# Two attention layers on one core: first half of the next queries ahead of a step's first score, maxima at scores 1 to 8, residual additions behind all maxima

## The chip, the core and the metric

One Trainium2 chip, one of its NeuronCores. The engines are TensorE (PE, matmuls), VectorE (DVE), ScalarE (ACT), GpSimd (POOL) and SyncE (SP, which here only issues DMAs). The metric is the time of one execution on the device in microseconds; lower is better.

## The reference

Four layers over x, which is 4 x 1024 rows of 256 numbers, each added to x behind a layer norm: a cross-attention over 77 context rows with a mask and 16 heads, a mixture of six small experts, a second cross-attention over the same context with one key and value head for all 16 query heads, and a feed-forward layer. Cut to the two attentions, which the change touches, the masked one first, then the scores of the second:

```python
q = (h @ Wq.T + bq).reshape(B, N, H, D).transpose(0, 2, 1, 3)
scores = jnp.einsum('bhnd,bhtd->bhnt', q, k) * scale + attention_mask[:, None, :, :]
attn = jax.nn.softmax(scores, axis=-1)
out = jnp.einsum('bhnt,bhtd->bhnd', attn, v)
return out.transpose(0, 2, 1, 3).reshape(B, N, C) @ Wo.T + bo

attn_score = jnp.einsum('bhid,bjd->bhij', qh, k) / np.sqrt(D_HEAD)
attn_prob = jax.nn.softmax(attn_score, axis=-1)
```

## The kernel before

**Tiling.** The 4096 rows of x are cut into 8 blocks of 512. Each attention is a loop of 8 steps G, one for a block: G = 0 to 7 is the masked layer (here also steps 0 to 7), G = 8 to 15 the second one. Between them the experts run, behind them the feed-forward layer. The order on each engine is written out by hand in one program for each engine, and the engines meet by semaphores.

**One step.** A step does 16 scores, one for a head. `score` (L383) multiplies keys by a stack of queries in SBUF, `qst`, which holds the high and low parts of the queries and, in two rows, the row maxima, so that the matmul gives scores with the maximum already taken off; the masked layer adds the mask by a second matmul (L399). ScalarE's `exp` (L297) follows each. After each group of four heads `weigh` (L402) multiplies by the values, eight matmul records in the trace, and `divide` (L330) on VectorE transposes the result and divides it by its denominator: L335, L338, L340. The fourth group of a step is weighed and divided in the next step. `fold` (L343) transposes a half of the heads, `lead_quotient` (ScalarE) and `rest_quotient` (GpSimd) split it into a high and a low part, and `output` (L412) multiplies it by Wo in twelve matmuls (L421), for two halves k of the block; `add` (L348) adds each to x. All that is work for the block p = G-1.

For the next block n = G+1 the same step prepares the stack. `queries` (L357) computes one half c of its queries in six matmuls (L135). It waits for the rest `xl` of the normalized input, both halves. ScalarE's `leading` (L283) takes the high part, VectorE's `rest` (L310) the low part, and SP copies both into `qst` (`stack_queries`, L242). Then the maxima: 16 units u, each one matmul (two in the masked layer, L371 and L374) of 128 queries by the keys of four heads (`max_unit`, L361), reduced by VectorE (`take_maxima`, L320, L327). The units share two banks, `X`:

```python
if u >= len(banks):
    pe.wait_ge(self.max_taken, 16 * G + u - len(banks) + 1)
```

When all 16 are reduced, TensorE transposes them (`turn_maxima`, L377), ScalarE copies them (`maxima`, L292) and SP copies them on into `qst` (`stack_maxima`, L253, qst<-mt). Score 0 of the next step waits for that DMA:

```python
if i == 0:
    pe.wait_ge(self.mt_stacked, 16 * (G + 1))
```

For the block after that, nm = G+2, VectorE takes the moments of its rows (`moments`, L87, at the start of a step), GpSimd the inverse root (`invert`), ScalarE normalizes (`norm`, at score 9), TensorE transposes (`turn`, L118, at scores 11 and 12, each behind the residual addition `att.added` that frees its bank `W`), ScalarE takes the high part (`lead`, L124), VectorE the rest (L130), which ends just at the step's end.

**Order before, TensorE.** score i; at i = 0 and 1 the queries' halves behind the score; at 1 the fourth weighing of p; at 3 to 10 two units each; at 8 and 9 the outputs; at 5, 9 and 13 the weighings; at 12 the transposition of the maxima; at 11 and 12 the input's. **VectorE:** moments, two rests of the queries, maxima 0 to 3, division 3 and fold 1 of p, maxima 4 to 9, division 0, maxima 10 and 11, the two additions, maxima 12 to 15, division 1, fold 0, two rests of the input, division 2. In step 11 (BLOCKS + 3) VectorE also prepares bias rows of the feed-forward layer (L1371 to L1380). In steps 9, 10, 12 and 13 ScalarE and GpSimd split weights of the feed-forward layer in passing (L1045, L1053). The last step of each layer has no queries and no maxima.

## Time and profile before

| | us |
|---|---|
| median of 3 runs (lowest, highest) | 865.36 (864.72, 866.4) |
| the profiled execution | 866.98 |
| its span in the profile | 865.2 |
| busy: PE, DVE, ACT, POOL | 774.8 (90%), 659.9 (76%), 520.1 (60%), 398.4 (46%) |

The kernel runs through the masked attention from about 41 to 232 us, the experts to about 440, the second attention to about 632 and the feed-forward layer behind it. A step of the masked layer takes some 26.3 us, one of the second some 23.4 to 24.5. In a timeline each row is an instruction or a run of equal ones: start, duration, engine, line, what it writes and reads, and in brackets how long its engine had been idle and what released it. Matmuls overlap: one of 512 columns starts every 0.23 us and is shown with 0.39 to 0.40; one that had to wait for its operands is shown longer. A number of bank or buffer is left out of the names; "bank" is PSUM.

### The profile page before, as it was taken

Reading aid. Unit: us, or ns where it says so; the run is one execution under the profiler, and the core shown is the slowest. Engines: PE = TensorE matmul, PEld = TensorE weight load, DVE = VectorE, ACT = ScalarE, POOL = GpSimd, SP = SyncE. Lnnn points to the kernel's source line nnn. Section 1 sums busy time; section 2 is a strip of 40 time slices with the busy share of each in tenths; the row PEclk is TensorE's granted clock in tenths of the full one; section 3 lists DMA queues with packets and bytes.
Section 4 is the critical chain, followed back from the end, with each engine's and each line's share of the span. In section 5 each row is a group of like instructions: output and inputs, shape, how many; then the busy total and the mean of one; then the engine's idle time right before and its main releaser. Section 6 shows DMA issues by size and latency. Waiting matters only on the chain.

```text
span 865.2 us, 13721 instructions
## 1 busy us (share of the span) xinstructions
PE 774.8 (90%) x4452; PEld 568.9 (66%) x4452; DVE 659.9 (76%) x1576; ACT 520.1 (60%) x942; POOL 398.4 (46%) x323
## 2 busy tenths in 40 slices
PE   4799999999899999999988988988879999899996
PEld 3456556666467787777754544554458888788885
DVE  7657877777768777877777888888777778787784
ACT  3455565555554455544446675666668787788774
POOL 5523322223233433443311221222159998988995
PEclk9999999999999999999988999999999999999999
DMA  6965643355200000001075446555000000000001
GB/s 216 159 164 109 146 78 72 74 107 102 70 0 1 2 3 5 2 1 50 15 97 70 59 60 110 88 75 75 3 1 1 25 1 26 25 25 2 25 25 50
DMA packets 24817, 48.01 MB, mean 55 GB/s; under 512 B 3655, under 2 KB 6856, under 8 KB 24234
## 3 DMA queue, kind: packets, MB, share of 16 engines
q1 hardware_dynamic: 23224, 46.02, 27.8%
q10 hardware_dynamic: 1522, 1.11, 0.4%
q8 instruction: 37, 0.61, 0.3%
q14 instruction: 34, 0.28, 0.1%
HBM read 11.47 MB, written 4.19 MB: 18 GB/s over the span
## 4 chain that ended last, share of the span: by engine, by line
PE 52%; DVE 18%; POOL 11%; issue 7%; ACT 5%; DMA 5%; POOLq 0%; ACTq 0%; DVEq 0%
PE bank L135 15%; PE bank L396 5%; PE bank L371 5%; PE bank L629 5%; PE bank L421 5%; DMA qst<-mt 4%; PE bank L407 4%; DVE mx L327 4%; POOL eex L508 4%; PE bank L777 4%; POOL fy L696 3%; POOL frise L689 3%; PE bank L399 2%; PE bank L121 2%; DVE x L597 2%
## 5 line engine op out<-in xcount | busy, mean ns | idle before, releaser
L301 ACT ACTIVATE pt<-bank 77x512 f32<-77x512 f32 x256 | 146.4, 589 | 123.5 <-PE bank L399 76.4
L327 DVE TENSOR_REDUCE mx<-bank 128x4 f32<-128x308 f32 x256 | 108.9, 471 | 30.3 <-PE bank L374 17.8
L396 PE MATMUL bank<-qst,l_kst 128*77 128x512 f32 (+1 forms) x256 | 106.7, 431 | 19.3 <-DMA qst<-mt 13.3
L696 POOL TENSOR_TENSOR fy<-fpart,fg 128x512 f32<-128x512 f32 x64 | 103.9, 1624 | 9.4 <-DVE fpart L737 4.8
L371 PE MATMUL bank<-l_kblk,qh 128*128 128x308 f32 x256 | 89.7, 366 | 12.0 <-DVE mx L327 9.8
L689 POOL TENSOR_TENSOR frise<-fg,fg 128x512 f32<-128x512 f32 x64 | 90.1, 1408 | 9.0 <-POOL fy L696 4.7
L103 POOL TENSOR_TENSOR rstd<-var,minus_half 128x4 f32<-128x4 f32 x32 | 33.2, 1039 | 127.6 <-DVE var L98 74.9
L396 PEld LDWEIGHTS bank<-qst,l_kst 128*77 128x77 f32 (+1 forms) x256 | 36.8, 148 | 83.2 <-issue 48.8
L277 POOL TENSOR_TENSOR ol<-ot,oh 128x512 fp32r<-128x512 f32 x32 | 43.0, 1345 | 94.2 <-ACT oh L306 62.1
L371 PEld LDWEIGHTS bank<-l_kblk,qh 128*128 128x128 f32 x256 | 49.3, 193 | 55.9 <-issue 46.8
L737 DVE SCALAR_TENSOR_TENSOR fpart<-ffixed,frise 128x512 f32<-128x512 uint16 x64 | 58.6, 915 | 33.0 <-POOL frise L689 32.8
L597 DVE SCALAR_TENSOR_TENSOR x<-bank,eweight,x 128x256 f32<-128x256 f32 x192 | 79.5, 475 | 4.4 <-PE bank L629 4.1
L777 PE MATMUL bank<-fw2h,fyh 128*128 128x256 f32 x256 | 72.3, 282 | 3.5 <-DVE fyl L743 3.5
L407 PE MATMUL bank<-pt,l_vall 128*32 128x512 f32 x512 | 69.4, 614 | 6.4 <-DVE ut L335 3.8
L113 ACT ACTIVATE xn<-x,shift,rstd 128x256 f32<-128x256 f32 x128 | 68.1, 590 | 11.6 <-POOL shift L105 11.6
L777 PE MATMUL bank<-fw2l,fyh 128*128 128x256 f32 x256 | 71.9, 281 | 0.0
L777 PE MATMUL bank<-fw2h,fyl 128*128 128x256 f32 x256 | 71.8, 281 | 0.0
L706 ACT ACTIVATE fg<-ffixed 128x512 f32<-128x512 int16 x64 | 40.4, 632 | 45.4 <-DVE ffixed L731 45.2
L629 PE MATMUL bank<-ew2h,ehh 128*128 128x256 f32 x192 | 56.6, 295 | 10.3 <-DVE x L597 10.3
L629 PE MATMUL bank<-ew2l,ehh 128*128 128x256 f32 x192 | 54.7, 285 | 0.0
L629 PE MATMUL bank<-ew2h,ehl 128*128 128x256 f32 x192 | 54.5, 284 | 0.0
L731 DVE TENSOR_SCALAR ffixed<-bank 128x512 int32<-128x512 f32 x64 | 43.7, 683 | 12.0 <-PE bank L135 11.9
(179 smaller groups left out, 2144.2 us busy)
## 6 DMA issues: line engine op xcount, KB each, us to landing
qst<-qh SPq DMA_DIRECT2D x64, 256.0 KB, 6.7
qst<-ql SPq DMA_DIRECT2D x32, 256.0 KB, 9.0
out<-x SPq DMA_DIRECT2D x8, 512.0 KB, 2.6
qst<-ml SPq DMA_DIRECT2D x8, 480.0 KB
x<-in_x SPq DMA_DIRECT2D x3, 1024.0 KB, 12.7
weights<-in_mlp_w SPq DMA_DIRECT2D x2, 1024.0 KB, 5.1
mraw<-in_mask SPq DMA_DIRECT2D x8, 154.0 KB
x<-in_x SPq DMA_DIRECT2D x2, 512.0 KB, 5.5
```

Source lines behind the costliest of these rows:

```text
L113: last = self.nc.scalar.activation(self.xn[:, t:t + 1, :], self.tile(n, t), ACT.Identity, bias=self.shift[:, t, :], scale=self.rstd[:, t, :])
L135: last = self.nc.tensor.matmul(out, w, a, start=(first and k == 0), stop=(k == len(ops) - 1))
L301: self.nc.scalar.activation(self.pt[0:T, i // 4 % 2, i % 4, :], self.bank_of(G, i)[0:T, :], ACT.Exp).then_inc(self.probs, 1)
L327: self.nc.vector.reduce_max(out, banks[u % len(banks)][:, 0:4 * T].rearrange("q (p par t) -> q p par t", p=2, par=2), AX.X).then_inc(self. ...
L371: last = self.nc.tensor.matmul(bank, self.qh[:, c, tile], keys, start=True, stop=not layer.masked)
L396: last = self.nc.tensor.matmul(out, layer.kst[rows, layer.stack(c * HC + 2 * k + par), b * T:(b + 1) * T], self.qst[rows, self.slot(G), c ...
L407: last = self.nc.tensor.matmul(self.U[32 * k:32 * k + 32, :], layer.vall[:, self.batch(G), layer.value(c * HC + 2 * k + par), :], self.pt[ ...
L597: last = self.nc.vector.scalar_tensor_tensor(tile, part, self.weight[:, g % 2, 2 * k + t, e:e + 1], tile, ALU.mult, ALU.add)
L629: last = self.nc.tensor.matmul(self.OUT[k][:, t * D:(t + 1) * D], a[:, e % self.R, tile], w[:, e, :], start=(j == 0), stop=(j == 2))
L689: self.nc.gpsimd.tensor_tensor(self.rise[:, k % 2, :], self.g1[:, k % self.R, :], self.g0[:, k % self.R, :], ALU.subtract).then_inc(self.r ...
L696: self.nc.gpsimd.tensor_tensor(self.y[:, k % 2, :], self.part[:, k % 2, :], self.g0[:, k % self.R, :], ALU.add).then_inc(self.y_ready, 1)
L777: last = nc.tensor.matmul(self.OUT[2 * (g % 2) + t // 2][:, t % 2 * D:(t % 2 + 1) * D], a[:, k % self.R, t * P:(t + 1) * P], w[:, c, :], s ...
```

## The change

The same instructions on the same data, in another order on three engines, in both layers:

- TensorE: `queries` c now stands ahead of score c instead of behind it (c = 0, 1). The units stand at scores 1 to 8 instead of 3 to 10, and ahead of the fourth weighing at score 1. The transposition of the maxima stands at score 10 instead of 12.
- ScalarE: `leading` stands ahead of the exponential of the same number, and `maxima` at 10 instead of 12.
- VectorE: maxima 0 and 1 stand between the two rests of the queries; maxima 4 and 5 between division 3 and fold 1; all of 10 to 15 behind division 0; and both residual additions behind all maxima.

SP's and GpSimd's programs are unchanged. The part of the masked layer; the second layer's is the same but for its names and limits:

```diff
@@ -1105,9 +1105,9 @@
                 for G in range(BLOCKS):
                     p, n, nm = G - 1, G + 1, G + 2
                     for h in range(H):
-                        att.exp(act, G, h)
                         if h < C and n < BLOCKS:
                             att.leading(act, n, h)
+                        att.exp(act, G, h)
                         if h == 3 and p >= 0:
                             if p == 0:
                                 act.wait_ge(kblk_more, H)
...
@@ -1276,23 +1276,24 @@
                     if n < BLOCKS:
                         for c in range(C):
                             att.rest(dve, n, c)
-                        att.take_maxima(dve, n, range(0, 4), att.X)
+                            att.take_maxima(dve, n, range(2 * c, 2 * c + 2), att.X)
                     if p >= 0:
                         att.divide(dve, p, 3)
+                    if n < BLOCKS:
+                        att.take_maxima(dve, n, range(4, 6), att.X)
+                    if p >= 0:
                         att.fold(dve, p, 1)
                     if n < BLOCKS:
-                        att.take_maxima(dve, n, range(4, 10), att.X)
+                        att.take_maxima(dve, n, range(6, 10), att.X)
                     else:
                         ex.split_w1(dve, ew1)
                     att.divide(dve, G, 0)
                     if n < BLOCKS:
-                        att.take_maxima(dve, n, range(10, 12), att.X)
+                        att.take_maxima(dve, n, range(10, 16), att.X)
                     if p >= 0:
                         for k in range(2):
                             att.add(dve, p, k)
-                    if n < BLOCKS:
-                        att.take_maxima(dve, n, range(12, 16), att.X)
-                    else:
+                    if n == BLOCKS:
                         ex.split_w2(dve)
                         ex.split_router(dve)
                     att.divide(dve, G, 1)
...
@@ -1456,16 +1458,16 @@
                     for i in range(H):
                         if G == 0 and i == HC:
                             pe.wait_ge(kst_in[1], 16 * 6)
-                        att.score(pe, l0, G, i)
                         if i < C and n < BLOCKS:
                             att.queries(pe, l0, n, i)
+                        att.score(pe, l0, G, i)
+                        if 1 <= i <= 8 and n < BLOCKS:
+                            if i == 1 and G == 1:
+                                pe.wait_ge(kblk_more, H)
+                            for u in (2 * (i - 1), 2 * (i - 1) + 1):
+                                att.max_unit(pe, l0, n, u, att.X)
                         if i == 1 and p >= 0:
                             att.weigh(pe, l0, p, 3)
-                        if 3 <= i <= 10 and n < BLOCKS:
-                            if i == 3 and G == 1:
-                                pe.wait_ge(kblk_more, H)
-                            for u in (2 * (i - 3), 2 * (i - 3) + 1):
-                                att.max_unit(pe, l0, n, u, att.X)
                         if i in (8, 9) and p >= 0:
                             if G == 1 and i == 8:
                                 pe.wait_ge(wol_ready, 1)
@@ -1478,7 +1480,7 @@
                             att.output(pe, l0, p, i - 8)
                         if i in (5, 9, 13):
                             att.weigh(pe, l0, G, i // 4 - 1)
-                        if i == 12 and n < BLOCKS:
+                        if i == 10 and n < BLOCKS:
                             att.turn_maxima(pe, n, att.X[0])
                         if i in (11, 12) and nm <= BLOCKS:
                             if p >= 0:
```

## Rows read from the trace of the kernel before

**Rows 1.** The page's chain that ended last: share of the span by line

```profile
PE bank L135 15%; PE bank L396 5%; PE bank L371 5%; PE bank L629 5%; PE bank L421 5%; DMA qst<-mt 4%; PE bank L407 4%; DVE mx L327 4%; POOL eex L508 4%; PE bank L777 4%; POOL fy L696 3%; POOL frise L689 3%; PE bank L399 2%; PE bank L121 2%; DVE x L597 2%
```

**Rows 2.** Waits of 40 to 232 us: engine line waited for: us, times, longest

```profile
PE bank L396 <- DMA qst<-mt: 5.2, 7, 0.8
```

**Rows 3.** The waits, 445 to 632 us (second attention)

```profile
PE bank L396 <- DMA qst<-mt: 8.1, 6, 1.4
```

**Rows 4.** Timeline, TensorE, masked layer: start, us, engine, line, out<-in, count [idle before]

```profile
144.98 0.46 PE L396 MATMUL bank<-qst,l_kst 128*77 128x512 f32 x1 [0.75 <-DMA qst<-mt]
...
159.11 0.39 PE L416 MATMUL bank<-bias,ones 128*128 128x512 f32 x1
...
163.53 1.06 PE L407 MATMUL bank<-pt,l_vall 128*32 128x512 f32 x8
```

**Rows 5.** Timeline, VectorE, masked layer, the same step

```profile
143.39 0.69 DVE L130 TENSOR_TENSOR xl<-bank,xh 128x512 fp32r<-128x512 f32 x1 [0.26 <-ACT xh L126]
...
169.73 0.69 DVE L130 TENSOR_TENSOR xl<-bank,xh 128x512 fp32r<-128x512 f32 x1 [0.27 <-ACT xh L126]
```

**Rows 6.** Busy us (instructions) of each engine in one step, clock, DMA share, GB/s

```profile
564.65:588.03 23.38, 20.92 (x112) 11.75 (x112) 19.87 (x48) 15.47 (x30) 6.31 (x7) 1.00 0.53 70
```

**Rows 7.** Timeline, TensorE, one step of the second layer

```profile
564.65 0.46 PE L396 MATMUL bank<-qst,l_kst 98*77 98x512 f32 x1 [1.37 <-DMA qst<-mt]
...
575.49 0.76 PE L371 MATMUL bank<-l_kblk,qh 128*128 128x308 f32 x2
...
576.53 0.77 PE L371 MATMUL bank<-l_kblk,qh 128*128 128x308 f32 x2
577.14 0.28 PE L421 MATMUL bank<-l_woh,oh 128*128 128x256 f32 x1
...
580.97 1.07 PE L407 MATMUL bank<-pt,l_vall 128*32 128x512 f32 x8
```

**Rows 8.** The chain of that step in order: start us, us, what

```profile
561.69 2.92 DMA qst<-mt
...
565.12 1.38 PE bank L135 x6
```

**Rows 9.** Timeline, VectorE, the same step of the second layer

```profile
563.13 0.69 DVE L130 TENSOR_TENSOR xl<-bank,xh 128x512 fp32r<-128x512 f32 x1 [0.27 <-ACT xh L126]
...
564.76 1.14 DVE L340 TENSOR_TENSOR o<-ut,rden 128x256 f32<-128x256 f32 x1
565.83 1.40 DVE L90 BATCH_NORM_STATS2 stats<-x 128x6 f32<-128x256 f32 x4
...
567.83 0.68 DVE L317 TENSOR_TENSOR ql<-bank,qh 128x512 fp32r<-128x512 f32 x1
...
571.74 0.71 DVE L335 STREAM_TRANSPOSE ut<-bank 128x512 f32<-128x512 f32 x1
...
572.77 0.43 DVE L340 TENSOR_TENSOR o<-ut,rden 128x256 f32<-128x256 f32 x1
...
586.54 0.69 DVE L130 TENSOR_TENSOR xl<-bank,xh 128x512 fp32r<-128x512 f32 x1 [0.26 <-ACT xh L126]
```

**Rows 10.** TensorE in two stretches: busy us (instructions), granted clock, DMA share, GB/s

```profile
452.00:454.00 2.00, 2.00 (x10) 0.69 1.06 131
480.00:482.00 2.00, 2.00 (x9) 0.52 1.08 127
```

**Rows 11.** Timeline, TensorE, start of step 0

```profile
40.87 0.68 PE L396 MATMUL bank<-qst,l_kst 128*77 128x512 f32 x1 [4.22 <-issue]
```

**Rows 12.** Timeline, VectorE, before step 0

```profile
36.88 1.29 DVE L130 TENSOR_TENSOR xl<-bank,xh 128x512 fp32r<-128x512 f32 x2 [6.16 <-ACT xh L126]
```

**Rows 13.** Timeline, GpSimd, step 0

```profile
45.11 1.03 POOL L263 TENSOR_TENSOR mh<-mraw,zero 77x512 fp32r<-77x512 f32 x1
```

**Rows 14.** Timeline, TensorE, the starts of steps 8 and 9

```profile
445.20 0.43 PE L396 MATMUL bank<-qst,l_kst 98*77 98x512 f32 x1 [1.55 <-issue]
...
467.73 0.46 PE L396 MATMUL bank<-qst,l_kst 98*77 98x512 f32 x1 [1.34 <-DMA qst<-mt]
```

More of the change, by code:

```diff
@@ L1120, in _ @@
                             norm.norm(act, nm)
-                        if h == 12 and n < BLOCKS:
+                        if h == 10 and n < BLOCKS:
                             att.maxima(act, n, att.X[0])
@@ L1174, in _ @@
                     for h in range(H):
-                        att.exp(act, G, h)
                         if h < C and n < 2 * BLOCKS:
                             att.leading(act, n, h)
+                        att.exp(act, G, h)
                         if h == 3 and p >= BLOCKS:
@@ L1183, in _ @@
                             norm.norm(act, nm)
-                        if h == 12 and n < 2 * BLOCKS:
+                        if h == 10 and n < 2 * BLOCKS:
                             att.maxima(act, n, att.X[0])
@@ L1353, in _ @@
                             att.rest(dve, n, c)
-                        att.take_maxima(dve, n, range(0, 4), att.X)
+                            att.take_maxima(dve, n, range(2 * c, 2 * c + 2), att.X)
                     if p >= BLOCKS:
                         att.divide(dve, p, 3)
+                    if n < 2 * BLOCKS:
+                        att.take_maxima(dve, n, range(4, 6), att.X)
+                    if p >= BLOCKS:
                         att.fold(dve, p, 1)
                     if n < 2 * BLOCKS:
-                        att.take_maxima(dve, n, range(4, 10), att.X)
+                        att.take_maxima(dve, n, range(6, 10), att.X)
                     att.divide(dve, G, 0)
                     if n < 2 * BLOCKS:
-                        att.take_maxima(dve, n, range(10, 12), att.X)
+                        att.take_maxima(dve, n, range(10, 16), att.X)
                     if p >= BLOCKS:
@@ L1365, in _ @@
                             att.add(dve, p, k)
-                    if n < 2 * BLOCKS:
-                        att.take_maxima(dve, n, range(12, 16), att.X)
                     if G == BLOCKS + 3:
@@ L1559, in _ @@
                             pe.wait_ge(ex.added, ALL_EXP)
-                        att.score(pe, l1, G, i)
                         if i < C and n < 2 * BLOCKS:
                             att.queries(pe, l1, n, i)
+                        att.score(pe, l1, G, i)
+                        if 1 <= i <= 8 and n < 2 * BLOCKS:
+                            for u in (2 * (i - 1), 2 * (i - 1) + 1):
+                                att.max_unit(pe, l1, n, u, att.X)
                         if i == 1 and p >= BLOCKS:
                             att.weigh(pe, l1, p, 3)
-                        if 3 <= i <= 10 and n < 2 * BLOCKS:
-                            for u in (2 * (i - 3), 2 * (i - 3) + 1):
-                                att.max_unit(pe, l1, n, u, att.X)
                         if i in (8, 9) and p >= BLOCKS:
@@ L1575, in _ @@
                             att.weigh(pe, l1, G, i // 4 - 1)
-                        if i == 12 and n < 2 * BLOCKS:
+                        if i == 10 and n < 2 * BLOCKS:
                             att.turn_maxima(pe, n, att.X[0])
```

## The prediction

> **What bounds the kernel now.** I read the chain of work that ended last first: TensorE heads it by its matmuls, but the copy of the maxima into the query stack (qst<-mt) holds 4% of it and the maxima on VectorE (L327) another 4% [rows 1]. The waits then say what that copy costs: TensorE stood idle for it 7 times in the masked layer, 5.2 us in all, and 6 times in the second, 8.1 us [rows 2, 3]. So a step begins with 0.75 us (masked) or 1.37 us (second layer) of idle TensorE in front of score 0 [rows 4, 7]. That is what the change aims at. The busy times of one step of the second layer are to be read beside it: of 23.38 us VectorE works 19.87 and TensorE's "20.92" is stretched by matmuls that wait [rows 6]. VectorE has 3.5 us to spare in a step, and what a reordering is worth depends on where in the step they lie.
>
> **The head of a step.** The first half of the queries (L135, six matmuls, 1.38 us [rows 8]) needs only the rest of the normalized input, which VectorE ends at 563.13+0.69 = 563.82; score 0 starts at 564.65 [rows 7, 9]. With the queries first, TensorE starts at about 563.87 (0.05 from release to start, an estimate; bounds 0 and 0.2): 0.8 us earlier. In the masked layer it is 143.39+0.69 = 144.08 against 144.98 [rows 4, 5]: 0.85. The copy itself is issued two scores earlier, behind score 10, and 1.6 us of queries now run before score 0, so its 2.9 us [rows 8] are hidden: by the walk below unit 15 is issued at 15.2, the transposition of the maxima behind score 10 ends at 20.0, ScalarE's copy at 20.9, the transfer at 23.9, and score 0 wants it at 25.4. SP's queue does not oppose that: the copy stands behind the query copies and the mask load there, all issued in the step's first third. What is late next at the head is VectorE's rest itself, which a step's end sets.
>
> **The maxima at scores 1 to 8.** Each of the 16 units writes one of two banks and must wait until VectorE has reduced the unit two before. Where nothing else lies between, that loop of two units and a score takes 1.04 us (575.49 to 576.53), of which TensorE needs 0.24 for the score and 0.3 for the units [rows 7]. Before, 12 units precede the first output (577.14) and the last four lie behind outputs, where VectorE has had time and they go at TensorE's pace. After, all 16 precede it, without filler: queries, the fourth weighing of the step before and the first weighing lie among them, no output.
>
> I walk one step of the second layer, from its start 0 (queries first). TensorE: queries 1.39, score 0.24, queries, score, units 0 and 1 issued at 3.5. VectorE: it still divides the third group of the step (0.71+0.25+0.43 [rows 9], 1.4 in all, begun just before 0), to 1.2; moments 2.0 (565.83 to 567.83 [rows 9]), to 3.2; rest of the queries 0.6; so maximum 0 starts at 3.8, not at TensorE's pace. Then, each reduction some 0.4: 0 and 1 to 4.7; the other rest to 5.3; 2 and 3 to 6.1; the division of the fourth group, 1.4, to 7.4; 4 and 5 to 8.3; fold to 8.8; 6 and 7 to 9.7; 8 and 9 to 10.7. Units 8 and 9 could be issued at 9.4 and 9.8, and only behind them the first weighing (1.0 us): 10.3 to 11.3. VectorE's next instruction is the division of just that group, so it idles from 10.7 to 11.4, and divides until 12.8; units 12 and 13 wait for maxima 10 and 11 behind it. The last four reductions end in the 1.04 us loop, unit 15 is issued by 15.2, and the first output starts at 15.2. Before it started at 577.14-564.65 = 12.5 [rows 7]. From the output to the second weighing are two outputs and a score, 3.2 us: 18.4. From the second weighing to the last rest of the input were 587.23-580.97 = 6.26 us [rows 7, 9]; units 14 and 15 no longer lie in it (0.68): 5.6, which gives 24.0. So the period becomes 24.0 where it was 23.4: **0.6 slower**, though the head's wait is gone. The residual additions behind the maxima cost nothing themselves (0.7 each, VectorE is free then; the transposes that wait for them come 2.5 us later). Their former place between the maxima was the one that kept units 12 to 15 off TensorE's path.
>
> Where GpSimd works on weights at a step's start, VectorE's multiply takes 1.14 instead of 0.43 [rows 9]. Before, VectorE waited for unit 0 anyway and lost nothing; now the 0.7 us lie on the path, in four steps.
>
> The masked layer, the same walk: each unit has a second matmul, VectorE is 0.3 later at maximum 0 (moments start later behind a longer multiply) and 1.0 later at the division of the first group, and the first output starts at 16.5 against 159.11-144.98 = 14.1; weighing 20.3 against 18.55 [rows 4]. From there to the last rest were 170.42-163.53 = 6.89 [rows 4, 5], less 0.57 for two units: 26.6, against 26.3: 0.3 slower.
>
> **Single steps.** Step 0 gains: TensorE waited 4.22 us until 40.87 for the first maxima copy, while the rest of the next input was there at 36.88+1.29 = 38.17 [rows 11, 12]. The queries (2.6 us at the low clock) go into that wait. Their successors then wait for GpSimd's mask (45.11+1.03 [rows 13]), so 2.0 of the 2.6 stay. Step 8 has no outputs and no divisions of a step before; its units don't wait behind them, and it takes 19.5 where it took 467.73-445.20 = 22.5 [rows 14], 3.0 less (bounds 1 and 3.5: unit 15 ends at 13.6 and no output follows, the second weighing starts at 13.9, and 5.6 us later the rest is there). The last step of each layer has no maxima and starts with VectorE's chain, which is the later one now.
>
> **The clock.** The granted clock was 0.69 in 452 to 454 and 0.52 in 480 to 482 [rows 10], that is down to the lower level of 1.2 GHz, each time just behind a few microseconds in which TensorE did only scores and units at VectorE's pace. Steps of the same shape kept 1.00, so this stretch is at the edge. The change makes it 10 us long (5 to 15 in the walk) in six steps; I take four or five of them at 1.1, and 1.5 for step 8, which the sum below treats as if its clock were even. Its price: two microseconds at 0.52 lose 1.0 us of TensorE's work, and the edges of the window a little more: 1.1 each time. The Trainium skill (TensorE: Matmul & The Clock Gate, A second HAM failure mode: psum-queue depth-cycling) has the same thing: short idle times between groups that cycle through PSUM banks make the clock swing between its levels. By that page each of the six steps would pay, 877.
>
> **Sum**, against the profiled execution of 866.98 us (span 865.2; the median of the runs is 865.36, 1.6 less, and I move the sum onto it): step 0 -2.0; steps 1 to 6 6 x 0.3 = +2.0; step 7 +0.4; step 8 -3.0; steps 9 to 14 6 x 0.6 = +3.7, GpSimd 4 x 0.7 = +2.8, the step with the bias rows (its VectorE work now lies wholly behind the additions; bounds 0 and 1.5) +0.5, less 1.8 that these six already paid for one low clock (1.1) and once for GpSimd (0.7) = +5.2; steps 7 and 15 start from VectorE's rest, which is later than TensorE's last score by 0.1 to 0.7: +1.2 for 15. That is +3.8 with an even clock. Clock: 4.5 x 1.1 + 1.5 = +6.5. Together +10.3, from 865.4 to 875.7; the clock's part is bounded by 0 and twice this, and I take **874**, a little nearer to the even clock.
>
> **Rivals.**
> *Even clock.* The stretch holds weighings and queries, and five of this layer's seven steps with maxima stay at full clock today. Then only the walk counts: +3.8, 869 (867 to 871). 20%.
> *Faster: VectorE keeps pace.* If VectorE reaches the maxima before TensorE needs them, the whole idle of the head is earned and nothing is paid: 5.2 + 8.1 [rows 2, 3] and step 0's 2.0, 15 us: 850. It decides at the first weighing: if VectorE's division of that group ends before units 12 and 13 are due (11.9 in the walk, where I have 12.8). Part of it, a walk wrong by 1 us a step, gives 860. For it speaks that VectorE has 3.5 us to spare, against it that they come only behind the maxima. 17%.
> *Clock down twice a step.* The low clock also falls on both outputs (2.8 us of matmuls that double): another 1.5 in six steps, 883. 8%.
> *No change.* The head's gain and the stretch's loss cancel in both layers, 865.4 within 1.7. 7%.
>
> **Numbers.** My case has 48%: 874, by itself 871 to 879. Walk errors of 0.3 us in 13 steps make 4 us, the clock 0 to 9. Eight in ten: 861 to 882; what is left out is the full gain and the worst clock. About 0.2% (1.7 us) is what a measurement of this kernel tells from no change. Faster by more: 17% plus a little of the rest, 0.18; same 0.09; slower 0.73.
>
> **What would show it.** The wait for qst<-mt gone from TensorE in all steps (if not, the head is wrong). In the second layer a step of about 24.0 us, its first output 15.2 after its start, TensorE idle before units 6 and 12 with VectorE as releaser, VectorE idle before the transposition of the first group. Clock under 1 between the fifth and the eighteenth microsecond of several steps. If the step is at 22.5 or below with few idle times before L371, the walk of VectorE is wrong and the faster rival holds; if the steps are at 24 and the clock is even, 869.

## The result, and the profile after

The changed kernel takes 886.64 us (median of 4 runs, 885.62 to 887.29) against 865.04 us for the kernel before on the same chip: a ratio of 1.0245, 95% interval 1.0231 to 1.0258. The forecast was 874, 861 to 882: the direction was right, the loss was 2.4 times the forecast one (21.6 us against 9), and the time lies outside the range.

The page of the changed kernel, its span, busy times and chain:

```profile
span 884.6 us, 13721 instructions
...
PE 789.4 (89%) x4452; PEld 578.2 (65%) x4452; DVE 663.2 (75%) x1576; ACT 519.1 (59%) x942; POOL 397.0 (45%) x323
...
PEclk9899999999999999999887887878999999999999
...
PE 51%; DVE 21%; POOL 10%; issue 7%; ACT 7%; DMA 2%; SPq 0%; ACTq 0%; DVEq 0%; POOLq 0%
PE bank L135 14%; PE bank L407 6%; PE bank L371 6%; PE bank L629 5%; PE bank L421 5%; PE bank L396 4%; DVE mx L327 4%; PE bank L777 4%; POOL eex L508 4%; POOL fy L696 3%; DVE ut L335 3%; POOL frise L689 2%; PE bank L399 2%; PE bank L121 2%; DVE x L597 2%
```

The copy of the maxima, which held 4% of the chain before [rows 1], is gone from it: the change does what it says. The granted clock (PEclk, tenths) is 7 or 8 in nine slices in a row, from about 420 to 620 us, which is the second layer and what leads up to it. The waits of that layer, 440 to 655 us (engine, line, what it waited for: us in total, times, longest):

```profile
PE bank L371 <- DVE mx L327: 18.6, 20, 2.1
DVE x L352 <- PE bank L421: 18.4, 14, 1.9
...
DVE ut L335 <- PE bank L407: 16.3, 16, 1.8
...
PE bank L396 <- DMA qst<-mt: 0.4, 1, 0.4
```

The 8.1 us of [rows 3] are down to 0.4. In their place TensorE waits 18.6 us for VectorE's maxima (before: 6.8), and VectorE 16.3 us for a weighing (before: 2.9) and 18.4 us for an output (before: 11.3). Step by step (each window runs from the step's first query matmul to the next; us, busy time of each engine, granted clock, DMA share, GB/s), steps 9 to 13:

```profile
465.70:492.96 27.26, 23.75 (x113) 14.00 (x113) 20.06 (x48) 15.48 (x30) 5.02 (x5) 0.81 0.45 60
492.96:520.24 27.28, 23.79 (x113) 14.00 (x113) 20.06 (x48) 16.61 (x32) 6.42 (x6) 0.81 0.45 59
520.24:548.99 28.75, 23.88 (x113) 14.05 (x113) 22.74 (x54) 15.76 (x30) 5.15 (x5) 0.82 0.52 90
548.99:574.89 25.90, 22.35 (x112) 12.64 (x113) 20.08 (x48) 14.60 (x28) 5.02 (x5) 0.87 0.48 66
574.89:602.42 27.53, 24.03 (x113) 13.97 (x113) 20.57 (x48) 15.44 (x30) 6.30 (x6) 0.81 0.45 59
```

The kernel before needed 23.38 us at a clock of 1.00 for step 13 [rows 6]. VectorE's work is the same (20.57 against 19.87); the step is 4.2 us longer because of where it stands idle and how fast TensorE runs. TensorE's matmuls in step 13, which begins at 574.89 (start, duration, engine, line, operands, idle before and its releaser):

```profile
584.38 0.98 PE L371 MATMUL bank<-l_kblk,qh 128*128 128x308 f32 x2 [1.99 <-DVE mx L327]
...
586.66 1.93 PE L407 MATMUL bank<-pt,l_vall 128*32 128x512 f32 x8
...
592.70 0.42 PE L421 MATMUL bank<-l_woh,oh 128*128 128x256 f32 x1
...
596.69 1.06 PE L407 MATMUL bank<-pt,l_vall 128*32 128x512 f32 x8
```

and VectorE and GpSimd in the same step:

```profile
582.58 1.27 DVE L340 TENSOR_TENSOR o<-ut,rden 128x256 f32<-128x256 f32 x1
...
588.66 0.72 DVE L335 STREAM_TRANSPOSE ut<-bank 128x512 f32<-128x512 f32 x1 [1.41 <-PE bank L407]
...
582.30 1.26 POOL L277 TENSOR_TENSOR ol<-ot,oh 128x512 fp32r<-128x512 f32 x1 [1.98 <-ACT oh L306]
```

Read them together. GpSimd's rest of the quotient starts at 582.30, VectorE's multiply at 582.58, and the multiply takes 1.27 instead of 0.42. The maxima behind it are late, TensorE stands idle for 1.99 us ahead of unit 6, and behind that its clock is low:

```profile
584.00:588.00 4.00, 3.62 (x13) 1.49 (x13) 2.85 (x7) 1.11 (x2) 0.93 (x1) 0.53 1.06 127
588.00:592.00 4.00, 3.51 (x12) 1.74 (x8) 2.88 (x7) 1.71 (x3) 0.88 (x2) 0.50 0.51 59
592.00:596.00 4.00, 4.00 (x23) 3.86 (x23) 1.72 (x4) 1.23 (x3) 0.74 (x1) 0.69 0.02 4
```

0.50 is 1.2 GHz. The first weighing takes 1.93 us instead of 1.06, VectorE waits 1.41 us for it, and most of the first output runs at 0.42 a matmul instead of 0.28. This multiply is the fourth division's, and it takes 1.27 to 1.36 in all of steps 9 to 13. Before, it took 0.42 or 0.43 in each of them, by a narrow margin: in step 13 GpSimd's rest ran from 571.26 to 572.53 and the multiply began at 572.77 [rows 9]. After, measured from the step's start, the rest comes 0.8 us later and the multiply 0.4 earlier.

**Where the 19.4 us between the spans (884.6 and 865.2) are.** From the starts of the steps in both traces: steps 0 to 6 +0.8 (step 7 starts at 224.79 against 223.97); step 7 and the experts -2.4 (step 8 at 443.59 against 445.20); step 8 -0.4 (22.1 against 22.5); steps 9 to 14 +20.4 (163.9 against 143.5); the rest +1.0. In two of these stretches the kernel before ran at a low clock that its order doesn't explain. Its step 8 is

```profile
445.20:467.73 22.53, 18.99 (x81) 9.84 (x81) 15.47 (x40) 13.84 (x26) 1.99 (x5) 0.85 0.54 72
```

and the same second layer, in the run below that changes the masked layer alone, takes 20.08 us for step 8 (443.82 to 463.90) at a clock of 1.00. And from the queries of step 6 to the first ones behind the experts the kernel before takes 229.59 us, with a low clock at 234; the run that changes the second layer alone has the same masked layer and takes 228.11, with none.

### The profile page after: what moved, and what is told of

Same layout as the page of the kernel before. It is cut to its first block, busy times and chain, and to the rows that moved or that the text cites. A ratio compares the mean times of both kernels' runs of the same rounds, so it can differ in the third digit from the quotient of the medians.

```text
span 884.6 us, 13721 instructions
## 1 busy us (share of the span) xinstructions
PE 789.4 (89%) x4452; PEld 578.2 (65%) x4452; DVE 663.2 (75%) x1576; ACT 519.1 (59%) x942; POOL 397.0 (45%) x323
## 3 DMA queue, kind: packets, MB, share of 16 engines
q10 hardware_dynamic: 1522, 1.11, 0.4%
## 4 chain that ended last, share of the span: by engine, by line
PE 51%; DVE 21%; POOL 10%; issue 7%; ACT 7%; DMA 2%; SPq 0%; ACTq 0%; DVEq 0%; POOLq 0%
PE bank L135 14%; PE bank L407 6%; PE bank L371 6%; PE bank L629 5%; PE bank L421 5%; PE bank L396 4%; DVE mx L327 4%; PE bank L777 4%; POOL eex L508 4%; POOL fy L696 3%; DVE ut L335 3%; POOL frise L689 2%; PE bank L399 2%; PE bank L121 2%; DVE x L597 2%
## 5 line engine op out<-in xcount | busy, mean ns | idle before, releaser
L371 PE MATMUL bank<-l_kblk,qh 128*128 128x308 f32 x256 | 94.4, 405 | 29.9 <-DVE mx L327 27.0
L396 PE MATMUL bank<-qst,l_kst 128*77 128x512 f32 (+1 forms) x256 | 112.7, 449 | 0.6 <-DMA qst<-mt 0.4
L371 PEld LDWEIGHTS bank<-l_kblk,qh 128*128 128x128 f32 x256 | 55.3, 217 | 74.9 <-issue 62.1
L396 PEld LDWEIGHTS bank<-qst,l_kst 128*77 128x77 f32 (+1 forms) x256 | 38.9, 155 | 63.9 <-issue 32.6
L407 PE MATMUL bank<-pt,l_vall 128*32 128x512 f32 x512 | 75.1, 661 | 4.1 <-ACT pt L301 2.7
L335 DVE STREAM_TRANSPOSE ut<-bank 128x512 f32<-128x512 f32 x64 | 45.5, 711 | 25.8 <-PE bank L407 25.8
```

Source lines behind the costliest of these rows:

```text
L335: nc.vector.transpose(self.ut[:, q % 2, :], self.U[:, :]).then_inc(self.unfolded, 1)
L371: last = self.nc.tensor.matmul(bank, self.qh[:, c, tile], keys, start=True, stop=not layer.masked)
L396: last = self.nc.tensor.matmul(out, layer.kst[rows, layer.stack(c * HC + 2 * k + par), b * T:(b + 1) * T], self.qst[rows, self.slot(G), c ...
L407: last = self.nc.tensor.matmul(self.U[32 * k:32 * k + 32, :], layer.vall[:, self.batch(G), layer.value(c * HC + 2 * k + par), :], self.pt[ ...
```

## Experiments

The theories are these. **A**, the low clock is a large part of the loss. **B**, GpSimd beside the multiply causes the idle time and so the low clock. **C**, only the order and its waits count, and the low clock falls into time that TensorE would wait anyway. **D**, the first weighing stands behind too many units. Changes of all kernels are against the changed kernel unless it is said otherwise; ratios are against the kernel before, run beside each of them.

**Each layer alone.** The masked layer's or the second layer's loops taken from the changed kernel, the other's from the kernel before.

> The change in the masked layer alone, the second layer as before. In the traces the changed kernel reaches step 8 1.6 us earlier than the kernel before, and everything later is unchanged here. Both theories of the second layer give 863.5 (862 to 865). If the layers hang together (the masked layer's order decides how the second one starts), it comes out above 866.

> The change in the second layer alone. The stretch from step 8 to step 15 took 19.9 us more and the tail behind it 1.1 more; if that is all of the loss, 865.0 + 21.0 = 886 (884 to 888), and this and the run with the masked layer alone add up to the changed kernel (+21.6). If less than 883, the two layers' losses are not independent.

Measured: masked layer alone 863.98 us, ratio 1.0005 (0.998 to 1.003); second layer alone 885.65, 1.0245 (1.0208 to 1.0281). The loss is the second layer's; of the masked layer's the interval leaves at most 0.3%.

**The quotient's copies later.** In the second layer:

```
-                        if h == 3 and p >= BLOCKS:
+                        if h == 5 and p >= BLOCKS:
                             att.lead_quotient(act, p, 0)
-                        if h == 5 and p >= BLOCKS:
+                        if h == 6 and p >= BLOCKS:
                             att.lead_quotient(act, p, 1)
```

> The changed kernel, with ScalarE's first copy of the quotient moved from score 3 to behind score 5 and the second from score 5 to behind score 6 in the second layer, so that GpSimd's rest of the first quotient no longer runs beside VectorE's multiply of the fourth division (1.27 us there instead of 0.43). Theory A (the low clock follows from the long stretch of maxima at VectorE's pace, whatever the overlap): only 0.85 us x 6 steps come back, 881 (879 to 884), and the clock still falls for about 10 us a step. Theory B (the overlap makes the 2-us idle time that tips the clock): overlap and low clock both go, 0.85 + 2.0 to 2.5 in six steps, 868 (865 to 872). Theory C (the order of waits alone, the first weighing sets VectorE's division): nothing comes back, 886 (885 to 888).

Measured: 882.49, 1.0212 (1.0178 to 1.0246), an interval that meets the changed kernel's. In its step 13 (from 570.44) the overlap is gone and the idle time is shorter, but the clock still falls:

```profile
578.13 0.42 DVE L340 TENSOR_TENSOR o<-ut,rden 128x256 f32<-128x256 f32 x1
...
579.09 0.88 PE L371 MATMUL bank<-l_kblk,qh 128*128 128x308 f32 x2 [1.15 <-DVE mx L327]
...
581.36 1.86 PE L407 MATMUL bank<-pt,l_vall 128*32 128x512 f32 x8
```

B falls as the only cause of the clock: 1.15 us of idle time are followed by it too, and the steps with maxima behind step 8 have it at 0.81 to 0.94. As a wait B is right: the first weighing starts 10.9 us after this step's start instead of 11.8, and in steps 9 and 12, where nothing is low ahead of it, 10.2 instead of 11.3 and 11.4 (11.2 in the filled kernel below). The walk of the prediction had 10.3. The whole kernel gains less than the steps do: steps 9 to 14 take 157.9 us instead of 163.9, and from step 15 on it is 257.3 instead of 255.0. Why the last step is longer with late copies, no run shows.

**The clock priced.** One kernel fills the idle times of the changed kernel and touches no wait and no order: in the second layer score 4 is issued eight times and score 7 five times, with the same data into the same bank, and only the last one signals.

```
+        for _ in range({4: 8, 7: 5}.get(i, 1) if not layer.masked and G + 1 < 2 * BLOCKS else 1):
             last = self.nc.tensor.matmul(out, layer.kst[...], self.qst[...], start=True, stop=not layer.masked)
```

> The changed kernel with score 4 issued eight times and score 7 five times in the second layer, as filler of the 2.0 us and 1.2 us for which TensorE waits for VectorE there; no wait and no order is changed. Theory A (clock): the granted clock of the steps goes from 0.81 to 0.97 or more, the first weighing takes 1.06 us again instead of 1.93 and the outputs are 0.8 us shorter, steps of 25.3 to 25.8 instead of 27.3, total 874 (871 to 878). Theory D (waits): the steps stay above 26.5, 880 to 887.

Measured: 875.83, 1.0117 (1.01 to 1.0134), that is 10.8 us below the changed kernel (11.1 by the ratios) although TensorE does more. Its steps 9 to 13:

```profile
465.51:490.36 24.85, 22.77 (x124) 13.29 (x124) 20.09 (x48) 15.28 (x30) 5.08 (x5) 1.00 0.50 66
490.36:515.19 24.83, 22.77 (x124) 13.29 (x124) 20.08 (x48) 16.50 (x32) 6.45 (x6) 1.00 0.50 65
515.19:542.52 27.33, 23.98 (x123) 13.82 (x123) 22.81 (x54) 15.75 (x30) 5.15 (x5) 0.94 0.56 94
542.52:568.40 25.88, 23.97 (x123) 13.82 (x123) 20.19 (x48) 14.47 (x28) 5.07 (x5) 0.93 0.48 67
568.40:593.67 25.27, 23.12 (x123) 13.34 (x123) 20.59 (x48) 15.42 (x30) 6.34 (x6) 1.00 0.49 65
```

and from step 13 a filler, the first weighing, the first output and the second weighing (the weighing's line is L408 here, the output's L422):

```profile
575.51 1.99 PE L397 MATMUL bank<-qst,l_kst 98*77 98x512 f32 x8
...
579.99 1.07 PE L408 MATMUL bank<-pt,l_vall 128*32 128x512 f32 x8
...
584.77 0.28 PE L422 MATMUL bank<-l_woh,oh 128*128 128x256 f32 x1
...
587.96 1.06 PE L408 MATMUL bank<-pt,l_vall 128*32 128x512 f32 x8
```

In step 13 the clock is 1.00, the weighing takes 1.07 and the step 25.27 where it took 27.53; steps 9 and 10 fall by 2.4 each and step 14 by 2.1. That is A, and against C: the low clock is worth 2.1 to 2.4 us in a step where the fillers hold it off. In steps 11 and 12 it still fell, for a shorter time, behind idle times of no more than 0.5 us, and they gain 1.4 and nothing. So 10.8 us is what the fillers won back, and not quite the whole price. B's other half stays true: the multiply of the fourth division still takes 1.29 to 1.38 here.

**Fillers that priced it badly.** Two earlier ones: every unit of the second layer's steps issued twice, and the four matmuls of the first weighing issued a second time ahead of units 6 and 7.

> The changed kernel, but each unit of maxima of the second layer's steps is computed twice by TensorE into the same bank (the second time with the same data), as filler: 16 more matmuls of some 0.17 us a step, in a stretch where TensorE waits for VectorE anyway. The six late steps now take 25.9 to 28.8 us at a granted clock of 0.81 to 0.87. Theory A (the clock falls because TensorE has too little to do in that stretch, and this costs some 3 us a step): the clock of a step rises to 0.95 or more and the step falls to 24.5 to 25.5, total 870 (866 to 875), although TensorE does more work. Theory C (the clock is incidental, waits and order set the step): at least 886, up to 890 for the added matmuls.

> Control of the filler: the run with the head alone (maxima at scores 3 to 10, clock about 0.98 there) with each unit of the second layer's steps computed twice. If the doubling gains only through the clock, there is nothing to gain here: 859 plus what of 16 x 0.17 = 2.7 us a step isn't hidden (0 to 1.5), 859 to 868. If doubling is a gain by something else (the order of banks, waits), it comes out below 857.

> A price for the low clock alone: the changed kernel, with the four matmuls of the first weighing issued a second time, as filler, ahead of units 6 and 7, into the same bank and with no signal to anyone; the real weighing stays behind units 8 and 9 and overwrites them. No wait or order of the others changes, only TensorE's idle time of 2 us falls to about 1. Theory A (the idle time tips the clock, and the clock is worth 1.7 to 2.5 us a step: weighing 1.93 instead of 1.06, outputs 0.8 more, units more): granted clock of a step 0.95 to 1.00, steps of 25.3 to 25.8, 875 (871 to 878). Theory D (the clock is a small part): 880 to 886. If the clock stays at 0.81 with the filler, the filler says nothing of the price.

Measured: doubled units 885.74, 1.0218 (1.0189 to 1.0248), with the clock of steps 9 to 14 at 0.94 but their length 26.7 to 28.2; the control (the kernel with the head alone, below, and doubled units) 862.41, 0.9949 (0.9932 to 0.9965), its step 9 24.03 against 23.34: doubling costs 0.7 us a step by itself in that order. In the changed order, where more units run at the pace of the maxima, it may cost more: two units and a score follow each other there in 1.19 us instead of 1.04. Weighing twice 881.18, 1.0174 (1.0143 to 1.0205): in step 13 the first weighing is back at 1.06 us, but the clock now falls behind the second idle time (1.16 us ahead of unit 12) and lies on the outputs. Both missed what A had expected, and by themselves they speak against it. They are weak evidence, since the clock wasn't held throughout in either; the run above, which shortens both idle times to under 0.5 us and adds only a few matmuls, held it in four of six steps.

**The first weighing earlier.** In the second layer, behind score 4 and ahead of units 6 and 7; then the same with the later copies of the quotient; then that with score 7 issued five times.

```
+                        if i == 4:
+                            att.weigh(pe, l1, G, 0)
                         if 1 <= i <= 8 and n < 2 * BLOCKS:
...
-                        if i in (5, 9, 13):
+                        if i in (9, 13):
                             att.weigh(pe, l1, G, i // 4 - 1)
```

> The changed kernel, with the first weighing of each step of the second layer ahead of units 6 and 7 (behind score 4) instead of behind units 8 and 9. In the changed kernel TensorE stands idle for 2 us in front of unit 6, and the weighing it could do there comes 2.3 us later (11.8 us after the step's start; 8.0 in the kernel before), with VectorE idle for 1.4 us in front of the division that it feeds. Theory D (moving the maxima ahead put ten units instead of six in front of the first weighing, and so delayed VectorE's first division and all behind it): the weighing starts at about 8, the 1.4 us of idle VectorE go, and with a filled gap the clock stays up too: steps of 24 to 24.8 us, 869 (866 to 873). Theory A alone (clock): the gap is filled as well, 872 to 876. Theory C (VectorE's sum of work sets the step whatever the order): 883 to 887.

> Both edits: the first weighing ahead of units 6 and 7, and ScalarE's copies of the quotient at scores 5 and 6, so that GpSimd doesn't run beside the fourth division. Theory D: as the run with the early weighing, less the overlap of 0.85 us in six steps: 865 (861 to 869). If the overlap no longer lies on the path once the weighing is early (TensorE bound there), both are equal within 1.5 us.

> The kernel with the early weighing and the late copies of the quotient (876.5 us; steps of the second layer 24.2 to 25.9 us, with TensorE idle for 1.15 us ahead of units 12 and 13 and a granted clock of 0.87 to 0.93), with score 7 issued five times in place of once in the second layer, as filler of that idle time; nobody waits for score 7 in it. Theory A: the clock stays at 1.00 and each step with maxima falls by 0.9 (those at 0.93) to 1.9 us (those at 0.87), 869 (867 to 872). Rival: another engine's chain sets these steps and the low clock only fills TensorE's slack: 874 to 878.

Measured: 884.52, 1.021 (1.0182 to 1.0238); 876.54, 1.0117 (1.0085 to 1.015); 867.76, 1.0023 (1.0013 to 1.0034). The first alone brings 2 us (3 by the ratios, with intervals that meet) where 18 were expected: VectorE's 1.41 us of idle time are gone and the units end 1.7 us earlier, but the low clock then falls on the outputs instead of on the weighing (step 13 26.99 against 27.53). With both waits and the clock mended, steps 9 and 13 are about where they were before (24.5 and 23.4) or below:

```profile
465.47:488.71 23.24, 21.52 (x117) 12.28 (x117) 19.05 (x48) 15.29 (x30) 5.31 (x5) 1.00 0.53 70
...
559.95:583.71 23.76, 21.94 (x116) 12.32 (x116) 19.62 (x48) 15.43 (x30) 6.57 (x6) 1.00 0.52 69
```

So D and the overlap are right as waits: 8.1 us together with the clock held (875.83 to 867.76). Without any filler each alone is worth 2 to 4 us, but both together 10 (886.64 to 876.54, 11 by the ratios), as much as the fillers alone. The low clock is shorter then too (0.87 to 0.93 in these steps instead of 0.81 to 0.87). Which part of the 8.1 is whose was not measured. In steps 8 to 14 the gain is larger, 162.7 us against 175.1; from step 15 on 4.5 us are lost (259.3 against 254.8), and no run says why.

**Maxima at scores 2 to 9.**

```
-                        if 1 <= i <= 8 and n < 2 * BLOCKS:
-                            for u in (2 * (i - 1), 2 * (i - 1) + 1):
+                        if 2 <= i <= 9 and n < 2 * BLOCKS:
+                            for u in (2 * (i - 2), 2 * (i - 2) + 1):
```

(and so in the masked layer)

> The changed kernel with the maxima at scores 2 to 9 instead of 1 to 8, in both layers: the last two units now stand behind the first output, with the second output right behind them, and the fourth weighing stands ahead of all units. Theory A: the stretch of units without other work is 2 us shorter and holds an output, so the clock falls for less or not at all, and VectorE is less late at the first ones: second-layer steps of 24 to 25.5 us, total 866 (860 to 872). Theory C: 1 us less of idle time a step at most, 878 to 882.

Measured: 886.6, 1.0229 (1.0209 to 1.0249): nothing gained, against A's 866. Its step 13 has a wait of 2 us in another place:

```profile
592.27 0.98 PE L371 MATMUL bank<-l_kblk,qh 128*128 128x308 f32 x2 [2.09 <-DVE mx L327]
```

That is unit 12, 15.2 us into the step; now GpSimd's work on the weights (590.19, 1.26 us) runs beside the first division's multiply (1.36 us), and the outputs run at the low clock. But only step 13 has it. In the other steps from 9 to 14 the longest idle time ahead of a unit is 1.16 us, the fourth division's multiply is at 0.42 or 0.43, and the clock is at 0.76 to 0.93 all the same. So neither a shorter stretch of units nor a clean fourth division keeps the clock up.

**The head alone.** Against the kernel before: in both layers only these, on TensorE and in the same way for the leading parts and exponentials on ScalarE.

```
-                        att.score(pe, l1, G, i)
                         if i < C and n < 2 * BLOCKS:
                             att.queries(pe, l1, n, i)
+                        att.score(pe, l1, G, i)
```

> The kernel before, with nothing but the queries put ahead of scores 0 and 1 on TensorE and their leading parts ahead of the exponentials 0 and 1 on ScalarE, in both layers; maxima at scores 3 to 10, additions and the turn of the maxima where they were. If the head's gain and the early maxima's loss are separate things (my walk): 0.8 us in each of 12 or 13 steps and 2.0 in step 0 come off, 853 (851 to 857), and TensorE's wait for the copy of the maxima is gone. If VectorE's or another chain sets the period anyway: 861 to 866, with the 0.8 us found again as idle TensorE ahead of maxima or outputs.

> The kernel before with the queries and leading parts alone moved, once more, for the interval: between 0.990 and 0.996 of the kernel before (856 to 862).

Measured: 858.86 us, 0.994 (0.9916 to 0.9965), and again 860.26, 0.994 (0.992 to 0.9961): 0.6% faster than the kernel before, clear of noise. The gain is where it was expected, 0.73 us in step 13 and 0.8 in a masked step, but it is 5 us, not 12. In both profiles a part is lost again around the step with the bias rows: TensorE waits 2.3 us for VectorE near the end of step 11, the clock falls behind that, and the queries of step 12 run at the low clock (step 12 25.33 and 24.12 us against 23.53 before, where the same wait was followed by no fall). In the first profile step 8 takes 19.76 us, in the second 22.40, with the same instructions:

```profile
438.99:458.75 19.76, 16.70 (x80) 8.58 (x80) 14.54 (x39) 14.13 (x26) 1.30 (x3) 1.00 0.63 83
...
439.37:461.77 22.40, 19.61 (x80) 9.39 (x81) 14.58 (x39) 14.26 (x26) 1.86 (x5) 0.85 0.56 73
```

The clock is what differs: 2.6 us in one step, without any filler.

**The additions.** The head alone, and the residual additions behind all maxima; TensorE's order stays.

```
-                        att.take_maxima(dve, n, range(10, 12), att.X)
+                        att.take_maxima(dve, n, range(10, 16), att.X)
                     if p >= BLOCKS:
                         for k in range(2):
                             att.add(dve, p, k)
-                    if n < 2 * BLOCKS:
-                        att.take_maxima(dve, n, range(12, 16), att.X)
```

> The run with the head alone, and in addition the residual additions behind all maxima on VectorE; TensorE's order stays (maxima at scores 3 to 10). By my prediction the additions' place between maxima 10/11 and 12 to 15 kept units 12 to 15 off TensorE's path, so moving them is a part of the loss only together with the early maxima: alone it gains or loses less than 0.3 us a step, 857 to 861 beside 859. Rival: the two transpositions that wait for the additions come 0.4 to 0.8 us later in each step: 864 to 867.

Measured: 874.09, 1.0082 (1.0062 to 1.0102), 12.3 us above the head alone by the ratios; a few of them may be step 8's clock, which is 0.79 in this profile (23.84 us against 19.76 and 22.40). The rival was right, and more than that: a masked step takes 26.55 instead of 25.50, step 13 23.73 instead of 22.65, and TensorE waits for the additions:

```profile
PE bank L121 <- DVE x L352: 9.0, 7, 1.9
...
588.28 0.66 PE L121 MATMUL bank<-ident,xn 128*128 128x128 f32 x4 [1.18 <-DVE x L352]
```

In the changed kernel this wait isn't there, since unit 15 precedes the first output and VectorE is free when the outputs end. With the early maxima the additions can't stay where they were either: they wait for outputs that now stand behind units 12 to 15, whose maxima were behind the additions.

**The head with small fillers.** The head alone, score 9 five times in step 8, scores 4 and 6 twice in the later steps.

> The kernel with the head alone, and short fillers in the idle times of its second layer: score 9 five times in step 8 (ahead of 1.15 us of idle TensorE), scores 4 and 6 twice in each later step with maxima (ahead of 0.29 and 0.41 us). Theory A (idle times ahead of units start the low clock in this order too): all steps at 1.00, steps of 19.8 and 23.4 us, 856 (854 to 858), 1.1% under the kernel before. Rival (the low clock there comes by other means, at random): as before, 859 to 861, or more for the filler.

Measured: 857.87, 0.991 (0.9893 to 0.9926). It hits A's range, but its interval meets that of the head alone, and step 8 was at 0.92 and step 12 at 0.88 all the same. That these fillers add anything is not shown. Step 12's low clock begins near the end of step 11, 2 us behind TensorE's 2.3 us of waiting for VectorE there, which no filler covers; what starts the one of step 8 stays open.

## Why the prediction was wrong

Point by point, by its own steps.

- **The head of a step: right.** The wait for qst<-mt is gone. In the masked layer TensorE starts 0.06 us after the rest of the input (143.84 + 0.69, then 144.59). By itself the head gives 0.7 to 0.8 us a step.
- **The masked walk: right.** First output 161.10 - 144.59 = 16.5 (forecast 16.5), weighing 20.4 (20.3), period 26.75 (26.6). Steps 0 to 6 gave +0.8 where the terms said 0.0 (-2.0 and +2.0).
- **The second layer's walk at even clock: right but for one term.** In the run with the idle times filled, step 13's first weighing starts 11.6 us after the step's start (forecast 10.3), the first output 16.4 (15.2), the second weighing 19.6 (18.4), and the period is 25.27. The forecast was 24.0, plus 0.7 where GpSimd works at a step's start, as it does there (multiply 1.11): 24.7, with 11.0, 15.9 and 19.1 for the three. Steps 9 and 10, without that, take 24.85 and 24.83. What is missing is 0.6 to 0.9 a step: **the failed step is the division of the fourth group, taken at 1.4 us**. That was its duration where it stood before [rows 9]; the walk placed it anew and did not ask what GpSimd does then. It works on the rest of the first quotient, in every step from 9 to 13, and a margin of 0.24 us was all that had kept the two apart. The multiply takes 1.26 to 1.36 instead of the 0.43 in that 1.4, in all six steps: 0.85 each, some 5 us. The run with the later copies bears this out: with the multiply back at 0.42 the first weighing starts 10.2 us after the start of steps 9 and 12, where the walk had 10.3 and the changed kernel has 11.3 and 11.4. No run has this division clean and the clock held with nothing else changed.
- **The GpSimd term was given to the wrong place.** I took four steps with the longer multiply at their start; of steps 9 to 14 only 13 and 14 have it (1.11; 0.42 in the other four), the two that also had it before (1.14). It is 0.7 us each, some 1.4 us too much.
- **The low clock: mechanism right, term mis-sized.** Forecast 4.5 steps at 1.1 us and 1.5 for step 8, 6.5 in all, of which about 5 are in the 874. Measured: 10.8 us, and 2.1 to 2.4 in a step where the fillers held it. I had taken the length of the low stretch from the kernel before, about 2 us a time [rows 10]; after, it lasts some 10 us (a clock of 0.81 over 27.3 us) in five steps and 7 in step 12, so all six have it. Each low microsecond is cheaper than I thought, 0.23 us instead of 0.5 (2.4 over 10); that TensorE waits for VectorE in many of them would explain it, but was not taken apart. The Trainium skill's rule (TensorE: Matmul & The Clock Gate, A second HAM failure mode: psum-queue depth-cycling), by which each of the six steps would pay, agrees with that count: the clock is 0.81 to 0.87 in all six. The 877 that I worked out with it were still too low, since the price of one was mine.
- **Step 8: the base was wrong.** Forecast -3.0 at even clock. Measured -0.4, with the clock at 0.85. The 22.5 us that I started from had been run at 0.85 as well (the row above); the same second layer takes 20.08 at 1.00. So at even clock the forecast of 19.5 was a gain of 0.6 and not of 3.0. In the changed order no profile has this step at 1.00 without added matmuls; with doubled units it is 21.31 there and with the fillers 21.91. With the maxima at scores 2 to 9, at 1.00, it took 19.77.
- **Between step 7 and step 8** the changed kernel gained 2.4 us that no term had. Before, the clock was 0.79 from 232 to 240 us; after, it is 1.00 there. About 1.5 us of it differ from one execution to the next: between the queries of step 6 and the first ones behind the experts the kernel before takes 229.59 us and the run with its masked layer 228.11, and the head alone takes 228.71 in one profile and 230.23 in the other, the longer ones each with a low clock there.
- **The additions cost nothing:** right in the changed kernel, wrong as a general statement (12 us when moved without the maxima).
- **The rivals.** The even clock (869) is near the 867.8 of the run with the clock held and the fourth division clean, but that run also has its first weighing early, so it is no test of it. The rival with the clock down twice a step (883) had 8% and came nearest. It was right in saying that the outputs also run low, and I gave it too little because the low stretches of the kernel before were short.

In sum, by stretches: in steps 9 to 14 the forecast had +10.2 us (5.2 at even clock and 5.0 for the clock) and the traces have +20.4. The filled kernel splits that: its steps 9 to 14 take 153.2 us, so the fillers win back 10.7 and 9.7 remain. The clock's term missed by some 5.7 and the walk by some 4.5, in which the 5 us of the fourth division stand against the 1.4 too much for GpSimd at the start. Elsewhere the forecast missed by +0.8 (steps 0 to 6), -2.8 (step 7 and the experts) and +1.1 (step 8). The rest is that I took 874 for a sum of 875.7, and that the medians differ by 2 us more than the two profiled executions.

## What to carry to other kernels

A work item moved by a microsecond meets other neighbours: before its old duration is used, look at what every other engine does at the new time. Where TensorE follows another engine with short idle times in between, price the lower clock by how long it lasts after the change, not by what it lasts today. Before a step's old time is used as a base, look at the clock at which it was run. And take a change apart: here one part of it gains 0.6%, and the rest costs three percent.

## What the runs showed of the hardware

- **The granted clock fell behind idle times of 1.15 to 2 us among short matmuls**, and in step 13 of the changed kernel it came back after 10 us, in the first output. It isn't a rule for one idle time: in steps 11 and 12 of the filled kernel the clock fell behind idle times of under 0.5 us, while step 8 with the maxima at scores 2 to 9 (1.15 us of idle time) and step 14 with the weighing twice (0.92 and 1.16) stayed at 1.00. The masked layer, in the same order but with a second matmul in each unit, stays at 1.00 in steps 1 to 6 (TensorE idle 0.78 us ahead of unit 6). Useless matmuls in the idle times, 11 of 0.23 us in a step, made the kernel 10.8 us faster.
- **A low clock that is moved isn't gone.** With the first idle time half filled (weighing twice) it fell behind the second in steps 10, 12 and 13; with the weighing early it fell on the outputs.
- **The same program takes one step in 19.76 or in 22.40 us**, and what the rows of the two show is a granted clock of 1.00 and of 0.85 (so too 22.53 and 20.08 for the second layer of the kernel before). So one profile of a step doesn't tell what the step takes.
- **GpSimd beside VectorE's multiply:** 0.42 alone, 1.26 to 1.38 beside GpSimd's subtraction of 1.26 to 1.29. In step 13 the multiply started 0.28 us behind it and ended 0.29 us behind its end. Two of VectorE's reductions, which read PSUM, take 0.87 beside GpSimd (591.29, GpSimd from 591.47 to 592.74) as without it. The Trainium skill (SBUF — State Buffer, SBUF: two separate sides) has this as a lock held for a whole instruction, between a GpSimd operation and a VectorE operation with two SBUF inputs; the traces agree, by these numbers.
